# Turning attention probabilities with VectorE, from scores laid out in column quarters

## The reference

```python
q = einsum('btc,hc->bth', x, Wq); k = ...; v = ...
scores = einsum('bth,bsh->bts', q, k) * C ** -0.5
scores = where(tril(ones((T, T))), scores, -inf)
out = einsum('bts,bsh->bth', softmax(scores, axis=-1), v)
```

## Time and profile before

| | |
|---|---|
| median of three runs | 2917.45 us |
| the profiled execution | 2912.74 us, span 2910.8 us |
| PE busy, MATMUL records | 2692.5 us (93%), 18974 |
| DVE busy, instructions | 1887.0 us (65%), 7229 |
| ACT busy | 1786.9 us (61%) |
| POOL busy | 1757.3 us (60%) |
| mean granted clock of TensorE | 0.972 |

### The profile page before, as it was taken

One profiled execution on the slowest core, in us unless ns is written; L12 is line 12 of the kernel. 1 busy time (PEld: TensorE's weight loads), 2 busy tenths in 40 slices (PEclk: granted clock), 3 DMA queues, 4 the chain that ended last, 5 costly groups with the idle time before them and its releaser, 6 DMA issues. The chain is left out here.

```text
span 2910.8 us, 53258 instructions
## 1 busy us (share of the span) xinstructions
PE 2692.5 (93%) x18974; PEld 2108.2 (72%) x18974; DVE 1887.0 (65%) x7229; ACT 1786.9 (61%) x4118; POOL 1757.3 (60%) x1837
## 2 busy tenths in 40 slices
PE   5688999999999999999999999999999998999775
PEld 3466787778777887778777887778777886787543
DVE  3467665867577665867577666867587656665324
ACT  3455666666676676666676676666676666665420
POOL 5777775776477756775477756775477656730000
PEclk8799999999999999999999999999999999999897
DMA  6445334633265324633265324633354323422397
GB/s 185 119 148 138 113 111 130 165 109 103 81 161 143 107 82 132 164 111 97 88 163 139 108 82 134 162 116 91 95 158 146 104 85 106 122 55 91 112 398 306
DMA packets 220067, 382.71 MB, mean 131 GB/s; under 512 B 44425, under 2 KB 130377, under 8 KB 219291
## 3 DMA queue, kind: packets, MB, share of 16 engines
q0 software_dynamic: 89856, 255.58, 30.1%
q1 hardware_dynamic: 125787, 108.75, 12.5%
q10 hardware_dynamic: 4160, 14.98, 1.3%
HBM read 316.77 MB, written 62.39 MB: 130 GB/s over the span
## 5 line engine op out<-in xcount | busy, mean ns | idle before, releaser
L533 POOL DMA_INDIRECT shared<-pair_table,idx x1800 | 1733.7, 963 | 833.0 <-issue 527.6
L1145 PEld LDWEIGHTS bank_o<-vals,prob_t 128*128 128x128 f32 x5200 | 633.7, 192 | 130.3 <-ACT prob_t L580 65.3
L1145 PE MATMUL bank_o<-vals,prob_t 128*128 128x128 f32 x5200 | 662.2, 276 | 31.5 <-ACT prob_t L580 31.5
L580 ACT ACTIVATE prob_t<-bank_r 128x512 f32<-128x512 f32 (+3 forms) x728 | 383.7, 548 | 474.1 <-PE bank_r L1132 473.3
L835 DVE CUSTOM_DVE_ANT_0 prob<-bank_r,mask 128x512 f32<-128x512 f32 (+3 forms) x728 | 449.2, 628 | 303.9 <-PE bank_r L1123 301.6
L1123 PE MATMUL bank_r<-keys,qt 128*128 128x512 f32 (+3 forms) x1456 | 635.7, 553 | 0.0
L825 DVE SCALAR_TENSOR_TENSOR shared<-shared,wb 128x128 f32<-128x128 f32 x1800 | 516.8, 347 | 163.8 <-ACT shared L561 163.0
L561 ACT ACTIVATE shared<-shared,wa 128x128 f32<-128x128 f32 x1800 | 561.6, 392 | 46.5 <-DMA shared<-pair_table,idx 46.5
L1112 PEld LDWEIGHTS bank_r<-convw_t,smp_t 128*128 128x128 f32 x3600 | 446.0, 195 | 56.5 <-issue 36.2
L1112 PE MATMUL bank_r<-convw_t,smp_t 128*128 128x128 f32 x3600 | 479.1, 279 | 1.1 <-ACT smp_t L566 1.1
L1132 PE MATMUL bank_r<-ident,prob 128*128 128x128 f32 x2600 | 383.1, 274 | 13.8 <-ACT prob L658 13.8
(11 more groups left out here) (158 smaller groups left out, 2198.2 us busy)
## 6 DMA issues: line engine op xcount, KB each, us to landing
shared<-in_dram SPq DMA_DIRECT2D x32, 1024.0 KB, 17.9
shared<-pair_table,idx POOLq DMA_INDIRECT x1800
pair_table<-rows_out SPq DMA_DIRECT2D x112, 256.0 KB
t<-in_dram SPq DMA_DIRECT2D x48, 256.0 KB, 4.1
t_dram<-t SPq DMA_DIRECT2D x48, 256.0 KB
shared<-in_dram SPq DMA_DIRECT2D x7, 1568.0 KB
stage<-t_dram POOLq DMA_DIRECT2D x8, 832.0 KB, 8.0
pm_dram<-logit SPq DMA_DIRECT2D x8, 800.0 KB
```

The lines of the kernel that those rows point to most:

```text
L533: pool.indirect_dma_start(g[t % RING][:, n, :], None, pair_table[b % 2], bass.IndirectOffsetOnAxis(ap=idx[:, b % 2, i * TAPS + n:i * TAPS ...
L580: act.activation(prob_t[q % 3][:, 0:w], ring_bank(("prob", t, c))[:, 0:w], ACT.Copy)\
L1145: last = pe.matmul(attn_ps, prob_t[q % 3][:, n * P:(n + 1) * P], vals[:, slot(tb, at), :], start=(at == 0), stop=(at == ti))
```

## The change

Tiles 4 to 24 of each image (21 tiles, `WIDE`) take another way; tiles 0 to 3 keep the old one.

- Scores of a wide tile come as 16 small products per chunk: queries in four blocks of 32 (`n`), keys in four sets (`m`): set `m` holds keys 32 m to 32 m + 31 of every 128. The product of block `n` and set `m` goes to partitions 32 m and up, columns `n * w/4` and up. A bank then holds, in each quarter of its partitions, one key set against all queries, so that 32 x 32 block transposes alone put keys on the partitions.
- DVE reduces a bank to four maxima (one per query block), after adding the mask on the last 128 keys in PSUM. ACT copies the scores to `prob` (`copy_scores`).
- The maximum over the four key sets lies across partitions: DVE makes `wmax`, PE transposes it (`cross`) at the end of the step, DVE takes the maximum over the sets and negates it (`neg`), PE spreads it to all partitions with four small products (`back`) at the start of the next step, and DVE copies it to `nmax`.
- ACT's exponential is four instructions, one per block, without a sum.
- DVE turns the probabilities into `prob_t` with one block transpose per chunk (`turn_blocks`). PE's transposes, and ACT's copies out of their banks, are gone for these tiles.
- The values get a 129th column of ones, so `attend` makes the row sum too, for all tiles.

```diff
@@ DVE
+                if is_wide(t):
+                    bank = ring_bank(("score", t, c))[:, 0:w].rearrange("p (b k) -> p b k", b=BLKS)
+                    if c == chunks_in(t) - 1:
+                        link(dve.tensor_tensor(bank[:, :, w // BLKS - BLK:], bank[:, :, w // BLKS - BLK:], mask_wide, ALU.add))
+                    dve.tensor_reduce(cmax[t % 2][:, c, :], bank, AXX, ALU.max).then_inc(score_ev, 1)
+                    return
...
+            def turn_blocks(t, c):
+                k0, w = chunks_of(t % TILES)[c]
+                q = CHUNKS_BEFORE[t] + c
+                after(exp_done, t + 1)
+                after(attended, q - 2)
+                if c == 0 and not is_wide(t - 1):
+                    after(prob_ev, q)
+                dve.transpose(prob_t[q % 3][:, 0:w].rearrange("p (j b q) -> p b j q", b=BLKS, q=BLK),
+                              prob_blocks(t, k0, w).rearrange("p b (j k) -> p b j k", k=BLK)).then_inc(prob_ev, 1)
...
             for step in range(END):
                 b, s = image_of(step)
                 ts, v, t = step - LAG_S, step - LAG_V, step - LAG_T
+                if is_wide(v):
+                    after(back_mm, wide_before(v + 1))
+                    after(exp_done, v - 1)
+                    dve.tensor_copy(nmax[v % 2][:], ring_bank(("back", v, 0))[:, 0:BLKS]).then_inc(max_done, 1)
...
                 for use in misc_at(step, "E") + misc_at(step, "F"):
                     keep_misc(use)
+                blocks = list(range(chunks_in(v))) if is_wide(v) else []
+                if blocks:
+                    turn_blocks(v, blocks.pop(0))
                 if step < ALL:
...
+                if blocks:
+                    turn_blocks(v, blocks.pop(0))
                 pieces = list(range(PIECES)) if step + 1 < ALL else []
                 for c in inner_rounds(step):
+                    if blocks:
+                        turn_blocks(v, blocks.pop(0))
                     if c + 2 < chunks_in(ts):
                         keep_scores(ts, c + 2)
                     if chunks_in(v) >= 4 and c >= 2 and pieces:
                         add_second(step + 1, pieces.pop(0))
                 if 0 <= ts < ALL:
...
+                    if is_wide(ts):
+                        after(cross_mm, wide_before(ts))
+                        dve.tensor_reduce(wmax[:], given, AXX, ALU.max).then_inc(wide_max, 1)
...
                 for p in pieces:
                     add_second(step + 1, p)
+                if is_wide(ts):
+                    after(cross_mm, wide_before(ts + 1))
+                    after(back_mm, wide_before(ts))
+                    dve.tensor_reduce(neg[:], ring_bank(("cross", ts, 0))[0:BLKS, 0:P].rearrange("b (i q) -> b q i", i=BLKS),
+                                      AXX, ALU.max, negate=True).then_inc(crossed, 1)
@@ PE
+                    if is_wide(ts):
+                        bank, cols = ring_bank(("score", ts, c)), w // BLKS
+                        sets = key_chunk(tb, k0, w).rearrange("p (j i k) -> p i j k", i=BLKS, k=BLK)
+                        for n in range(BLKS):
+                            for m in range(BLKS):
+                                last = pe.matmul(bank[m * BLK:(m + 1) * BLK, n * cols:(n + 1) * cols].rearrange("q (j k) -> q j k", k=BLK),
+                                                 qt[k % 2][:, at + n * BLK:at + (n + 1) * BLK], sets[:, m], start=True, stop=True)
+                        last.then_inc(scored, 1)
+                        return
...
+                def cross():
+                    free_ring(("cross", ts, 0))
+                    after(wide_max, wide_before(ts + 1))
+                    pe.transpose(ring_bank(("cross", ts, 0))[0:BLKS, 0:P], wmax[:], ident[:]).then_inc(cross_mm, 1)
+
+                def back():
+                    use = ("back", v, 0)
+                    free_ring(use)
+                    after(crossed, wide_before(v + 1))
+                    for m in range(BLKS):
+                        last = pe.matmul(ring_bank(use)[m * BLK:(m + 1) * BLK, 0:BLKS], neg[:], ident[0:BLKS, 0:BLKS],
+                                         start=True, stop=True)
+                    last.then_inc(back_mm, 1)
...
+                if is_wide(v):
+                    back()
                 if step < ALL:
                     for p in range(PIECES):
                         turn_samples(p)
...
                 if rounds.stop - 1 < chunks_in(v):
                     attend(rounds.stop - 1)
+                if is_wide(ts):
+                    cross()
                 for use in misc_at(step, "L"):
                     fill_misc(use)
@@ ACT
+                    if is_wide(v):
+                        after(score_copied, wide_scores_before(v + 1))
+                        rows = prob_blocks(v, 0, (v % TILES + 1) * P)
+                        for k in range(BLKS):
+                            last = act.activation(rows[:, k, :], rows[:, k, :], ACT.Exp, bias=nmax[r][:, k:k + 1])
...
                 if step < ALL and not samples_first:
                     for p in range(PIECES):
                         keep_samples(step, p)
+                for c in range(min(chunks_in(step - LAG_S), 3)):
+                    copy_scores(step - LAG_S, c)
```

More of the change, by code:

```diff
@@ L55 @@
 MIDDLE = 12 * P
+BLK = 32
+BLKS = P // BLK
+WIDE = frozenset(range(4, TILES))
 END = ALL + 16
@@ L145, with is_wide, wide_before @@
     CHUNKS_BEFORE.append(CHUNKS_BEFORE[-1] + chunks_in(_t))
+def is_wide(t):
+    return 0 <= t < ALL and t % TILES in WIDE
+def wide_before(t):
+    return sum(is_wide(u) for u in range(t))
 def rows_of(step):
@@ L166, in ring_order @@
         ts, v = step - LAG_S, step - LAG_V
+        if is_wide(v):
+            order.append(("back", v, 0))
         if step < ALL:
@@ L174, in ring_order @@
         order += misc_at(step, "F")
-        order += [("prob", v, c) for c in range(min(chunks_in(v), 2))]
+        turned = 0 if is_wide(v) else chunks_in(v)
+        order += [("prob", v, c) for c in range(min(turned, 2))]
         for c in inner_rounds(step):
-            order += [("prob", v, c + 1)] if c + 1 < chunks_in(v) else []
+            order += [("prob", v, c + 1)] if c + 1 < turned else []
             order += [("score", ts, c + 2)] if c + 2 < chunks_in(ts) else []
             order += misc_at(step, "M") if c == 1 else []
+        if is_wide(ts):
+            order.append(("cross", ts, 0))
         order += misc_at(step, "L")
@@ L386, in emptied, with prob_start, prob_blocks, wide_scores_before @@
             after(misc_ev_d if use[0] in MISC_BY_DVE else misc_ev_a, MISC_COUNT[use])
+        def prob_start(t):
+            return 0 if t % 2 == 0 else 2 * NP - P - (t % TILES + 1) * P
         def prob_at(t, k0, w):
-            start = 0 if t % 2 == 0 else 2 * NP - P - (t % TILES + 1) * P
-            return prob[:, start + k0:start + k0 + w]
+            return prob[:, prob_start(t) + k0:prob_start(t) + k0 + w]
+        def prob_blocks(t, k0, w):
+            start, n = prob_start(t), t % TILES + 1
+            return prob[:, start:start + n * P].rearrange("p (b k) -> p b k", b=BLKS)[:, :, k0 // BLKS:(k0 + w) // BLKS]
+        def wide_scores_before(t):
+            return sum(chunks_in(u) for u in range(t) if is_wide(u))
         def ring_bank(use):
@@ L990, in free_ring @@
                         after(score_ev, CHUNKS_BEFORE[t] + n + 1)
+                        if is_wide(t):
+                            after(score_copied, wide_scores_before(t) + n + 1)
+                    elif what == "cross":
+                        after(crossed, wide_before(t + 1))
+                    elif what == "back":
+                        after(max_done, t + 1)
                     elif what == "conv":
@@ L1032, in fill_misc @@
                     for k in range(m):
-                        last = pe.transpose(bank[:, k * P:(k + 1) * P], vals[:, at + k, :], ident[:])
+                        last = pe.transpose(bank[:, k * P:(k + 1) * P], vals[:, at + k, 0:P], ident[:])
                 elif what == "vals":
@@ L1071, in _ @@
             fill_misc(("gstat", 0, 0))
-            after(zeroed, 6)
+            after(zeroed, 7)
             after(setup_ev, 1)
@@ L1167, in _ @@
                     products(2)
-                if chunks_in(v) >= 2:
+                if turned >= 2:
                     turn_prob(1)
@@ L1171, in _ @@
                 for c in rounds:
[L1172 removed]
+                    if c + 1 < turned:
                         turn_prob(c + 1)
@@ L1482, in shape_constants @@
     mask = np.zeros((P, CHUNK + P), np.float32)
-    mask[:, CHUNK:] = np.where(np.arange(P)[None, :] > np.arange(P)[:, None], NEG, 0.0)
+    row, col = np.arange(P)[:, None], np.arange(P)[None, :]
+    mask[:, CHUNK - P:CHUNK] = np.where(col > row, NEG, 0.0)
+    key, query = row // BLK * BLK + col % BLK, col // BLK * BLK + row % BLK
+    mask[:, CHUNK:] = np.where(key > query, NEG, 0.0)
     of = np.arange(P) // (C // GROUPS)
```

103 lines of the change are left out of this document (61 added, 42 removed).

## The result

The changed kernel takes 3310.91 us (median of 4 runs, 3310.66 to 3313.48) against 2918.72 beside it, a ratio of 1.135 (interval 1.133 to 1.137). Slower was right, and the time lies in the stated range of 3010 to 3350, though above the forecast's own 3060 to 3280; the loss is 392 us where 258 were forecast. The profiled execution took 3311.13 (span 3309.3), to be set against the 3173 of the sum.

A forecast was written before the change was run, and what follows sets the result against it. PE's work sets the time, with DVE right behind it. An image goes from 326 to 361 us; +280 over eight images, less 20, gives 2912.7 + 260 = 3173, stated as 3175; own range 3060 to 3280, whole range 3010 to 3350.

The forecast's parts named there:

- second halves: Wide steps, convolution add to the crossing product (`crossed`): 4.3 to 9.0 us by chunks of the turned tile.
- The ring of two halves: PE waits at `back` for DVE's `neg`, so each half step lasts as long as its slower engine; chance 0.68.
- Image 361: One steady image takes 361 us instead of 326, +35.
- first halves: Wide steps, `back` to convolution add: 8.7 us in 11 steps with a normalisation block, 7.1 in 10 without.
- nine adds in 2.54: DVE's nine `add_second` in a second half take 2.54 us, counted as overlapped work (0.88 + 0.91 + 0.86).
- Step 10: The second half of step 10 of an image takes 4.8 us.
- DVE's operations: Block reduction and block transpose take 0.57 us each for 512 columns; some 51 us more DVE work an image.
- PE's sum: PE's removed and added work over all eight images: -275 + 11 + 20 + 71 + 74 = about -100 us.
- Rival (a): PE stays the bound and only the round trip at `back` is paid: 2870 us in total, faster; chance 0.10.
- (d): DVE's block transpose costs over 1 us; at 1.1 an image takes 390 us, the whole kernel 3410; chance 0.07.
- (b): Half of the 168 steps go like PE staying the bound, the others mildly: about 2915, no change; chance 0.05.
- (c): PE's granted clock falls to 0.91 in every image, slowing stretches PE decides: +14 x 8, 3285; chance 0.10.

The follow-up runs named there:

- quarter-turn run: Changed kernel with only the first 128 keys of each chunk of probabilities block-transposed on DVE: 3187.97 us, ratio 1.093 to the kernel before, 127 us less than the changed kernel.
- plain scores: Changed kernel with each chunk's 16 small score products replaced by one plain product of 128 rows: 3296.65 us, ratio 1.1297 to the kernel before.

## Why the prediction was right, and by how much it was not

The mechanism was right and the size a third short; the size failed in the second halves of the steps.

- **The ring of two halves.** Right, and shown: PE waits for `neg` (14 times in image 3), in step 94 the delay of `back` goes 1:1 into the step, and taking the maximum early gives 141 us back. Of the signs listed, the block transposes follow each other in 0.60 us, a group of four score records takes 0.11 to 0.12, DVE is at 76% of image 3 and PE at 86% (84 forecast); PE's largest wait is at the values products (14.3), and `back` is second (13.3), the other way round than listed.
- **Image 361, came out as 379.** The starts of the convolution adds and of `back` part image 3 as the forecast did:

  | part of image 3 (us) | forecast | measured |
  |---|---|---|
  | first halves, 21 wide steps | 175 | 176.1 |
  | second halves, 21 wide steps | 141 | 158.0 |
  | the four other steps | 46 | 45.0 |

  The whole miss lies in the second halves. The first halves worked out in numbers hold as well: 8.57 for 8.7 in step 95 and, from `back` at 1455.20 to the add at 1462.46, 7.26 for 7.3 in step 96. The second halves failed: 6.91 for 5.9, and 7.16 for 6.1 in step 95, where DVE waits 1.07 for ACT. The step of the forecast that failed is "nine adds in 2.54" as a plain sum of DVE's work: it priced DVE's wait for ACT's scalings at nothing and did not ask what is queued behind the new score copy. In the second halves of image 3 that wait is 12.4 us: 7.9 in eleven steps where the scalings stand behind a copy that waits for DVE, as in step 94, 3.1 in step 10, and 1.3 in step 17, where they stand behind a copy of queries that waits for PE. Beside it DVE waits 11.2 for `cross`, of which the forecast had only a part (0.4 in some steps, and 7 for steps 5 and 14 together); 4.3 of it is step 14. That an order with the scalings ahead of the copy would give it back was not tried, so what the queue costs in time is read from the trace and not shown by a run.
- **Step 10**, forecast 4.8 for its second half, took 9.0. ACT there in the changed kernel:

```profile
1301.25 0.81 ACT L625 ACTIVATE prob<-bank_r 128x512 f32<-128x512 f32 x2 [2.04 <-DVE cmax L894]
...
1302.43 1.14 ACT L727 ACTIVATE logit<-logit,route 64x1024 f32<-64x1024 f32 x1
...
1305.17 0.98 ACT L592 ACTIVATE shared<-shared,wa 128x128 f32<-128x128 f32 x3
```

  and PE behind it:

```profile
1305.32 1.16 PE L1267 MATMUL bank_o<-vals,prob_t 128*128 128x129 f32 x8 [3.18 <-ACT prob_t L611]
1306.41 4.14 PE L1120 MATMUL bank_r<-shared,offw_t 128*32 128x448 f32 x18
1310.48 0.27 PE L1246 MATMUL bank_r<-ident,wmax 128*4 128x128 f32 x1
```

  The copy waits 2.04 us for DVE, the routing exponentials (L727) stand behind it, the scalings behind them (2.99 us after the convolution add, 0.79 in the kernel before), and DVE's adds wait 3.12 us for these. PE stops for 3.18 and does its 18 offset records in 4.14 where the earlier trace rows have 2.46; `cross` stands behind them and `neg` behind `cross`.
- **DVE's operations.** 0.60 for 0.57, start to start: an estimated 5 us for 174 operations an image, and all of DVE's added work is 59 us for some 51, so 8 more. If about half of that reaches the time, as in the quarter-turn run, it is 4 of the 18 missed. That is an estimate; how the rest is split between ACT's queue, `cross` and the clock no run isolates.
- **PE's sum.** The terms for small scores and changes of mode hold (plain scores, above). Whole it shows 2759.8 and not about 2590: behind its stops the same records take longer (the rows at the end), which the forecast had not counted. By the granted clock (0.939 of the span against 0.972) PE was at half speed for some 400 us where it had been for 165; that makes at most an estimated 120 of the 170 us, and where the rest comes from is not shown.
- **Rival (a)**, PE stays the bound, fell at its own point: `neg` is not ready when PE comes to `back`, in 14 of the 21 wide steps of image 3. **(d)**, the dear transpose, fell at 0.69, and **(b)**, no change, with the result. **(c)**, the clock, came in part: 0.96 in image 3, not 0.91. Its 3285 is nearest to the measured 3311, but not for its reason: the first halves, where the clock was to cost, came out as forecast without it. The plain-score kernel speaks against the clock as the pace too: 0.925 over its span against 0.934, and 18 us faster. The Trainium skill (TensorE: Matmul & The Clock Gate, Part 1) has the gate open only under sustained work; the trace agrees so far: with PE's new stops the granted clock of image 3 fell from 1.00 to 0.96. What the clock cost in time no run isolates.
- **How near the size was.** +392 against +258: right in sign and in the place of the wait, a third short in size. That the time fell inside the stated range owes something to its width, since it reaches up to 3350 to hold (c) and a part of (d) as well.

## What to carry to other kernels

When work moves to another engine, list what stands behind each new instruction in that engine's queue, and who waits for that, also where the engine has much idle time: ACT is busy 56% of this span and DVE still waits for what stands in its queue. A maximum that must go over a second engine and back is worth taking as soon as its last input is there: the same instructions in another order gave 141 of the 397 us lost in that set. PE had only nine idle us an image, but DVE stood right behind it; taking work from the first of two engines that follow each other closely gained little here, and about half of the new work on the second was paid.

## What was not expected of the hardware

In image 3 all five stops of PE of 2.8 to 3.2 us were followed by a stretch at 1.2 GHz, though PE is busy before and after. PE of the changed kernel at the seam of steps 92 and 93:

```profile
1406.20 0.28 PE L1253 MATMUL bank_r<-ident,neg 4*32 4x4 f32 x8 [2.79 <-DVE neg L1029]
1406.42 2.18 PE L1203 MATMUL bank_r<-ident,shared 128*128 128x128 f32 x9
1408.53 4.80 PE L1227 MATMUL bank_r<-keys,qt 128*32 128x128 f32 x96
```

with the stretch around it:

```profile
1405.00:1415.00 10.00, 8.79 (x128) 7.97 (x129) 5.69 (x17) 5.05 (x10) 4.85 (x6) 0.66 0.25 70
```

The same nine and 96 records take 1.20 and 2.83 us behind the stop of 0.36 in step 94. The length of the stop does not decide alone: the stop of 1.96 us that ends at 1432.68 is followed by half clock too (26 `attend` records in 4.81 us, where 24 took 3.26 at 1415.85), the stop of 2.14 that ends at 1454.13 is not (nine and 96 records in 1.20 and 2.83 again). Where PE is what the step waits for, such a stop can cost twice: itself, and the slower records behind it.
